# A four-layer graph network on one core: the same steps, waits and buffers in another timetable

## The reference

```
L0: 8 heads of attention over the graph; logits q + k^T, masked by adj, leaky relu, softmax,
    out = sum over heads of attn @ (h @ fc_w) @ fp_w + h, then a sigmoid
L1: h' = x @ W.T + b;  e = h' A h'^T + its transpose;  softmax over masked e;  att @ h', relu, a gate
L2: 5 times: m = h @ weight[l];  agg = A @ m;  h = GRU(agg, h)
L3: a 17-tap convolution along the nodes;  exp(-dist) @ msg (dist from 3 features);  one GRU cell
```

## Time and profile before

| | |
|---|---|
| median of 3 runs | 2485.11 us (2477.29 to 2489.0) |
| profiled execution, its own time | 2485.19 us |
| its span, first to last instruction | 2483.4 us |
| busy: PE, DVE, ACT, POOL | 2191.5, 1635.4, 1551.5, 782.5 us |
| mean granted clock of PE | 0.945 of full speed |
| transfers | 65.44 MB, mean 26 GB/s |

### The profile page before, as it was taken

The page is one execution under the profiler, slowest core; times in us unless marked ns, Lnnn a source line. Parts: engine busy times, 40 slices in busy tenths (PEclk is TensorE's granted clock), DMA queues, the critical chain, the costliest instruction groups (busy, mean ns, idle before and its releaser), DMA issues.

```text
span 2483.4 us, 35526 instructions
## 1 busy us (share of the span) xinstructions
PE 2191.5 (88%) x12414; PEld 1800.1 (72%) x12414; DVE 1635.4 (66%) x4499; ACT 1551.5 (62%) x2980; POOL 782.5 (32%) x865
## 2 busy tenths in 40 slices
PE   4779999899999989999899989989998998999866
PEld 3658777686877868777686867768687776868644
DVE  3557676675767767576775758677576767767542
ACT  1738476583856748485684848668484765848432
POOL 0323324233332423334232333424233342423311
PEclk7979999999999999999999999999999999999988
DMA  3010101010010100000010010101001010100100
GB/s 109 18 39 1 34 26 35 26 31 14 17 35 26 35 26 18 22 22 35 26 35 26 1 35 27 35 26 35 26 1 35 26 35 26 35 9 1 35 5 5
DMA packets 46788, 65.44 MB, mean 26 GB/s; under 512 B 3728, under 2 KB 21392, under 8 KB 46352
## 3 DMA queue, kind: packets, MB, share of 16 engines
q1 hardware_dynamic: 46608, 63.16, 7.8%
HBM read 58.96 MB, written 4.19 MB: 25 GB/s over the span
## 4 chain that ended last, share of the span: by engine, by line
PE 60%; DVE 20%; ACT 9%; issue 8%; POOL 3%; DMA 0%; DVEq 0%; SPq 0%; ACTq 0%
PE banks L557 12%; PE banks L447 8%; PE banks L448 8%; PE banks L451 8%; PE banks L551 6%; PE banks L660 3%; PE banks L664 2%; PE banks L736 2%; DVE F L1217 2%; POOL rstd L365 2%; PE banks L623 2%; ACT F L856 2%; DVE F L1224 2%; PE banks L647 2%; DVE F L1204 1%
## 5 line engine op out<-in xcount | busy, mean ns | idle before, releaser
L557 PE MATMUL banks<-F,PT 128*128 128x128 f32 x4096 | 568.4, 283 | 37.6 <-DVE PT L1109 34.5
L557 PEld LDWEIGHTS banks<-F,PT 128*128 128x128 f32 x4096 | 527.8, 198 | 68.1 <-DVE PT L1109 47.0
L856 ACT ACTIVATE F<-banks,dcols 128x512 f32<-128x512 f32 x288 | 196.2, 681 | 162.7 <-PE banks L451 161.2
L395 POOL TENSOR_SCALAR U<-U,rden 128x512 f32<-128x512 f32 x192 | 151.4, 791 | 330.7 <-DVE rden L1099 330.7
L1109 DVE COPY PT<-banks 128x512 f32<-128x512 f32 x256 | 175.3, 685 | 62.2 <-PE banks L551 61.2
L395 POOL TENSOR_SCALAR tiles<-tiles,rden 128x512 f32<-128x512 f32 x192 | 132.8, 694 | 183.4 <-DVE rden L1099 183.3
L820 ACT ACTIVATE PT<-banks 128x512 f32<-128x512 f32 x256 | 150.9, 589 | 53.5 <-PE banks L551 51.9
L551 PE MATMUL banks<-ident,U 128*128 128x128 f32 x768 | 126.3, 295 | 65.0 <-POOL U L395 65.0
L1099 DVE RECIPROCAL rden<-den 128x1 f32<-128x1 f32 x512 | 80.2, 158 | 131.6 <-ACT tiles L808 64.5
L447 PE MATMUL banks<-R,WH 128*128 128x512 f32 x352 | 157.1, 446 | 3.7 <-DVE R L1289 2.9
L1204 DVE SCALAR_TENSOR_TENSOR F<-F 128x512 f32<-128x512 f32 x96 | 71.0, 739 | 133.0 <-ACT F L856 133.0
(11 more groups left out here) (217 smaller groups left out, 5574.2 us busy)
## 6 DMA issues: line engine op xcount, KB each, us to landing
adjN<-in_adj_dram SPq DMA_DIRECT2D x32, 1024.0 KB, 5.2
adjT<-in_adjt_dram SPq DMA_DIRECT2D x16, 1024.0 KB, 5.2
xin<-in_x_dram SPq DMA_DIRECT2D x18, 256.0 KB, 2.8
out_dram<-X SPq DMA_DIRECT2D x16, 256.0 KB, 2.3
F<-in_c2w_dram SPq DMA_DIRECT2D x1, 1088.0 KB, 7.7
F<-in_wraw_dram SPq DMA_DIRECT2D x1, 1024.0 KB, 9.4
PT<-in_fcw_dram SPq DMA_DIRECT2D x1, 512.0 KB, 3.8
PT<-in_fpw_dram SPq DMA_DIRECT2D x1, 512.0 KB, 4.6
```

The source lines that it names most:

```text
L395: pool.tensor_scalar(SC[s][h % RING][:, t, 0:NODES], SC[s][h % RING][:, t, 0:NODES], rden[s][:, t:t + 1], 1.0, ALU.mult, ALU.mult).then_in ...
L557: last = pe.matmul(B[s][:, 3, part(j)], PT[s][:, k, part(j)], G[s][:, k, h * DIM:(h + 1) * DIM], start=(h == 0 and j == 0 and k == 0), sto ...
L856: act.activation(F[s][:, tile, :], B[s][:, bank, :], func, bias=dcol(bias), scale=0.5)\
```

## The change

Only the numbers of `TURN` (and `GAP`, 140.9 to 140.868) are others. Every strand has the same steps, waits, buffers and instructions; what differs is how the strands of an engine are merged. Below, two of the entries:

```diff
-GAP = 140.9
+GAP = 140.868
...
-    ("Activation", "layer1"): (159.8, 166.7, 169.4, 172.2, 176.1, 177.1, 178.0, 179.8, 191.6, 193.3, 202.7),
+    ("Activation", "layer1"): (167.14, 169.55, 179.07, 179.07, 182.40, 182.40, 185.86, 186.07, 198.08, 200.57,
+        207.02),
```

More of the change, by code:

```diff
@@ L80 @@
        "h": 3, "y_banked": 3, "residual": 4}
-GAP = 140.9
+GAP = 140.868
 TURN = {
-    ("SP", "transfers"): (58.8, 132.9, 140.2, 201.0, 275.7, 335.9),
-    ("Pool", "inputs"): (5.0, 6.1, 57.9),
-    ("Pool", "normalized"): (61.9, 65.8, 67.3, 69.6, 77.1, 78.0, 80.1, 81.5, 87.6, 89.7, 92.2, 93.3, 94.7, 97.3,
[22 rows of a table removed]
-    ("Activation", "values"): (51.3, 54.8, 57.3, 58.7, 65.6),
-    ("Activation", "softmax"): (59.2, 60.0, 63.1, 64.2, 64.9, 66.1, 66.8, 68.5, 72.6, 73.4, 75.8, 76.5, 77.8, 78.9,
[4 rows of a table removed]
-    ("Activation", "tile_copies"): (72.1, 78.4, 86.4, 89.0, 100.1, 103.2, 111.9, 114.3, 121.2, 126.0, 129.8, 133.0,
[7 rows of a table removed]
[L126 to L132, removed]
-    ("DVE", "tile_copies"): (73.0, 76.4, 85.1, 89.6, 96.4, 101.6, 108.7, 113.0, 117.1, 123.2, 128.8, 132.4, 140.1,
[8 rows of a table removed]
@@ new lines @@
+    ("SP", "transfers"): (101.46, 205.40, 206.80, 206.80, 236.51, 372.69),
+    ("Pool", "inputs"): (0.00, 18.27, 120.88),
+    ("Pool", "normalized"): (35.91, 42.44, 42.47, 50.55, 52.44, 52.61, 53.08, 61.65, 67.02, 71.22, 75.33, 83.60,
[22 rows of a table added]
+    ("Activation", "values"): (57.80, 61.04, 61.04, 70.42, 76.00),
+    ("Activation", "softmax"): (66.86, 68.08, 70.19, 70.88, 72.38, 73.88, 74.05, 76.91, 79.45, 80.45, 80.45, 85.89,
[4 rows of a table added]
+    ("Activation", "tile_copies"): (84.84, 91.41, 95.94, 104.38, 110.79, 115.71, 124.10, 131.03, 137.05, 140.34,
[8 rows of a table added]
@@ new lines @@
+    ("DVE", "values"): (22.16, 28.65, 50.06, 52.03, 61.99, 74.14, 74.40, 80.55, 174.32),
+    ("DVE", "softmax"): (62.63, 62.63, 66.05, 73.76, 74.96, 75.36, 77.75, 78.89, 83.63, 85.30, 85.30, 86.72, 89.25,
+        89.39, 98.74, 98.74, 106.21, 106.21, 107.74, 107.87, 111.76, 113.49, 116.32, 118.61, 123.35, 129.90, 129.95,
+        133.04, 140.59, 148.87, 156.18, 165.13),
+    ("DVE", "denominators"): (76.16, 76.74, 79.46, 79.46, 86.39, 87.43, 88.01, 88.01, 88.01, 88.73, 99.72, 101.26,
+        107.21, 107.89, 108.39, 111.13, 111.37, 112.35, 116.57, 127.62, 133.55, 133.55, 133.55, 134.17, 143.48,
+        143.93, 151.72, 151.88, 158.19, 162.69, 170.87, 172.53),
@@ L142 @@
+    ("DVE", "tile_copies"): (82.63, 86.90, 88.48, 92.24, 105.52, 110.07, 115.34, 118.69, 130.70, 135.22, 150.12,
[8 rows of a table added]
 }
```

## The result

The change takes the median from 2481.2 us (four runs) to 2418.29 (2415.14 to 2424.35), a ratio of 0.9746 with a 95% interval of 0.9711 to 0.9781: 2.5% faster, some 63 us, where I had forecast 20. The direction was right and the size was not.

The account below looks back on a forecast made before the run. PE was taken to bound the kernel: of 146.3 us a period, 128 work, 12 waiting, 6 slow clock. Waits -0.2, clock -2.4 and +1.2 gave -1.4, over 14 periods -20 us, 2465 us; range 2422 to 2513.

Parts of the forecast that it names:

- head 6's T: PE's 4.04 us wait for POOL's normalization; reciprocals and normalizations moved ahead would cut 3.8 us of it a period.
- first `hp` product: PE's 1.98 us wait for DVE's scaled values; more cover ahead would leave 0.3, a gain of 1.7 us a period.
- turn: Turn of the period: z behind `hp` delays the cell, its transpose and layer 2's start; loss 3.9 us, 3.0 to 4.5.
- heads 6 and 7 beside layer 3: Copy for head 6's W behind an input's scaling, and two smaller delays of about 0.4 each: loss 1.9 us a period.
- ACT and DVE in the middle: Heads' and layer 2's steps merged anew; unpriced by the trace, taken as a 1.0 us loss, bounds 0 and 4.
- clock, all told: Slow clock changes by -2.4 us a period, with +1.2 lost again where a chain ends on PE at low clock.
- fill and end, once: The kernel's start and finish hold the same chains as a period; put at nothing, -3 to +3 us.
- z: ACT's gate in the turn waits for `hp` in full; were it free to pass, the total would be some 31 us lower.
- The W of head 6: PE waits longer for its copy, now behind an input's scaling on DVE: 0.7 to 2.6 us, taken as 1.1.
- The fuller clock: Rival: the full -4.9 us of clock a period counts and the 1.2 is not lost; -59 us, 2426; chance 0.20.
- ACT's order in the middle: Rival: layer 2's steps queue behind late exponents, 5 us of waits a period instead of 1.0; 2521 us; chance 0.22.
- nothing: Rival: the turn costs what head 6 gives, in waiting and clock; within 0.5%, 2485 us; chance 0.14.

Follow-up runs that it names:

- b_place2: The kernel before, with head 6's last two reciprocals moved ahead of DVE's residual and statistics, their normalizations ahead of POOL's rstd: 2489.76 us, ratio 1.004.
- a_place2_back: The changed kernel, with head 6's last two reciprocals back behind DVE's residual and statistics, their normalizations behind POOL's rstd: 2484.57 us, ratio 1.001.
- a_scale_late: The changed kernel, with DVE's scaling of the next graph's input put behind head 7's copies: 2393.52 us, ratio 0.965.
- a_z_first: The changed kernel, with layer 3's last gate z and the candidate put back ahead of `hp` on ACT: 2367.42 us, ratio 0.955.
- m_old_turn: The best version, with the turn (0 to 24.2 us) and both edges of the middle in the order of the kernel before: 2431.83 us, ratio 0.978.
- h_mid_late: The kernel before, with the middle and late part (24.2 us to the period's end) in the new order, turn and edges old: 2426.98 us, ratio 0.979.
- the best version: The changed kernel, with z and candidate ahead of `hp` on ACT and DVE's scaling of the next input behind head 7's copies: 2345.58 us, ratio 0.945.

## Why the prediction was wrong in size

By its own steps, per period, waits in us:

| term | forecast | measured |
|---|---|---|
| head 6's T | -3.8 | -4.0 |
| first `hp` product | -1.7 | -2.0 |
| layer 2's start | -2.0 | -1.8 |
| turn | +3.9 | +2.1 |
| heads 6 and 7 beside layer 3 | +1.9 | +2.2 |
| layer 1's transpose | +0.5 | +0.95 |
| ACT and DVE in the middle | +1.0 | about 0 |
| sum | -0.2 | -2.5 |
| clock, all told | -1.2 | -1.3 |
| a period, mean of thirteen | -1.4 | -2.9 |
| first of the fourteen | -1.4 | -8.5 |
| fill and end, once | 0 | -22.6 |

The waits are from the two sets of PE's timeline above and in the earlier trace rows; on the mean of thirteen periods their sum is -2.6 and the turn's +2.5. The clock is that of the table of experiments. With it the period would be 3.8 shorter; PE's work apart from both is recorded 1.0 us longer, within the 128.1 to 129.5 of all kernels.

Neither of the signs that were to show the prediction wrong came (the middle has under 3 us of waiting, the turn loses 2.1), and still it was.

**The fill and the end.** "The fill and end hold the same chains; I put them at nothing" is the step that failed most: 22.6 of the 48.7 us between the forecast of -20 and the span's -68.7; the first of the fourteen periods adds 7, the other thirteen 19. Of the 22.6 the fill has 17.1, good to some 4 us. Its rows were there to be read: 117.2 us with PE busy 84 and a clock of 0.83. The fill is no period with less in it. It has other waits, the T of heads 0 to 2, which no period has, and the new order among the heads takes 5 us off them. Why the end is 5.5 us shorter stays open.

**The turn.** The chain came as written: z behind `hp`, L491 waiting 2.04 (2.1 forecast), the mix behind the sum. What I had wrong is how its delay is paid. Counted from the `hp` on ACT (608.76, 719.15), layer 2's L484 starts 15.85 us later, where it was 11.79: 4.1 more, not 2.5. With the two G steps still to be done, 1.4, that is 5.5 us lost. But only 2.1 of it is waiting. The rest, 3.4, is PE at the low clock, for 6.8 us, shortly behind the wait of 2.04, in each of the thirteen periods (stretch 719.1 to 734.5, 0.78): its steps take longer and fill time that I had down as waiting. My sum had this delay as 3.9 of waiting and, besides, 1.7 and 1.2 for the clock on the same path, 6.8 us against 5.5. It is 1.8 of the 2.3 us by which the waits were out. The list of signs contradicts the sum here: it has L484 waiting 2.7, where the sum asks for 4.1; it waits 1.98.

**The middle.** A guess of 1.0 between bounds of 0 and 4; it was 0, PE busy 57.3 of 58.0 us. ACT at 54.6 of 58 had enough to spare. The rival that this would be worst is out.

**Head 6's T.** The amount was right in part by luck. The mechanism as I put it, two reciprocals and two normalizations that "could then run from about 694.7", left out that they need ACT's exponents, which ended at 696.96: by itself it gives 1.9 (b_place2) and nothing in time. In the change it is worth more, 3.0 (a_place2_back), since the merged order of the stretch around it is new too, which I had as "the masks also stand further ahead" and put at 0.2.

**The W of head 6.** I took 1.1 between 0.7 and 2.6; it was 2.25. The row of a 2.90 us scaling beside two POOL operations is the measured reason, and a_scale_late takes both away. The Trainium skill's page "SBUF — State Buffer", section "Who interferes with whom", has VectorE in a two-port mode and GpSimd lock each other out, which had made me write "nearer 2 than 1.1"; the trace agrees, 2.90 us beside POOL against 1.10 without.

**The clock.** It was to give back 2.4 less 1.2; over the period it went from 0.96 to 0.97. The 5.8 us lost became 4.5. By place, on the mean of thirteen: behind head 6's T and ahead of `hp` it gave back 2.6, where my terms come to 4.1 (4.9 less 0.8 for the W); the kernel before loses 2.2 behind head 6's T on the mean, not the 3.2 of the period that I had read. From `hp` to 30 us behind it the loss grew by 1.6, and I had 1.7.

**z.** The Trainium skill's page "TensorE: Matmul & The Clock Gate", section "Architectural detail: the array is 16× 32×32, not 1× 128×128", says that ScalarE and VectorE take their queue strictly in order. ACT's idle 3.81 us with z ready behind `hp` agree. I had the place at 31 us in all; a_z_first measures 51.

**The rivals.** The fuller clock was not it (4.5 lost, not 0.9). Its sum was wrong too: with "the full -4.9" it is 14 x (-0.2 - 4.9) = -71 us, 2414, and not 2426. Either is near the measured 2418 in its time alone. ACT's order in the middle and "nothing" are excluded.

## What to carry to other kernels

Read the fill and the end of a pipelined kernel in stretches of their own before putting them at nothing: with one graph in flight, the order among its own steps is the only cover, and fill and end gave a third of this gain. When a chain delays the bound engine itself, count how much later its end comes, once, and don't add the low clock on the same path to it: steps that run slower fill part of the wait. Before saying that a moved step can run from some time on, look at all of its inputs. And don't price an edit of an order by a run of it alone, nor sum such runs: the same turn was worth +44 and 0 us in two surroundings, and a stretch put in by itself keeps the old order at its edges, where waits of 2.0 and 2.7 us stood that neither whole version has. Undo it in the whole, and look at the timeline for the wait that an instruction standing in order behind an unready one makes; two such instructions moved by a few places gave 73 us more.

## What the hardware showed

- The granted clock isn't the same in every execution of one kernel: in 19 executions of the kernel before it was 0.940 to 0.951, and the time 2473 to 2491 us, the longer ones at the lower clock.
- Fewer waits did not make a shorter time. m_old_turn waits 9.9 us a period and h_mid_late 10.8, but the first loses 6.6 us to the low clock and the second 3.7, and their medians are 2432 and 2427 us. (m_old_turn's profiled execution was its slowest, 2444, so it may lose somewhat less in the others, under 1 us a period.)
- Four kernels with different waits (9.5, 9.8, 10.2, 10.8 us) have one period, 143.3 us, since the clock lost (4.5, 5.0, 3.9, 3.7) makes up for most of it. What in the pattern of waits decides where the clock falls stays open; no run here was made to tell it.
- A scaling of 1.10 us on DVE took 2.90 with two POOL operations running beside it, and none of the single ones without POOL beside it took over 346 ns.
- That the turn and the edges together gain 60 and 85 us beside the new middle and late part is measured, and half explained: without them the period of the best version is 6.6 us longer, 3.7 of waits (the K step's 2.04 and the W's 2.67, both at the edges, above all) and 3.5 of clock; why it falls more often there stays open too.
